# A gated recurrence on one core: the step re-ordered, and the update gate's products computed with the state as the stationary operand

## The reference

```python
vz, vr, vh = video @ C_z + b_z, video @ C_r + b_r, video @ C + b
def step(h, xs):                                  # layer 1, 256 steps in sequence
    xzt, xrt, xht = xs                            # seq @ W_z, seq @ W_r, seq @ W
    z = sigmoid(xzt + h @ U_z + vz)               # update gate
    r = sigmoid(xrt + h @ U_r + vr)               # reset gate
    hh = tanh(xht + r * h @ U + vh)               # candidate
    h_new = (1.0 - z) * h + z * hh
...
def step(h, z_t):                                 # layer 2, z_t is x + layer 1's output
    gate = sigmoid(h @ Wh.T + z_t @ Wz.T + b)
    h_new = tanh(h * (1.0 - alpha) + gate * z_t)
```

## Time and profile before

| | |
|---|---|
| Median of 3 runs | 990.21 us (986.84 to 991.89) |
| The profiled execution | 990.85 us, of which the span of the trace is 989.0 us |
| The 256 steps | from about 21 us to 612 us of the span |
| PE busy in 100 to 200 us | 99.05 us of 100 |
| DVE and ACT busy in the same stretch | 79.83 and 78.83 us |
| Mean step between 100 and 600 us | 2.252 us (222 steps in 500 us) |

### The profile page before, as it was taken

One profiled execution on the slowest core, in us unless ns is written; L12 is line 12 of the kernel. 1 busy time (PEld: TensorE's weight loads), 2 busy tenths in 40 slices (PEclk: granted clock), 3 DMA queues, 4 the chain that ended last, 5 costly groups with the idle time before them and its releaser, 6 DMA issues.

```text
span 989.0 us, 112546 instructions
## 1 busy us (share of the span) xinstructions
PE 943.0 (95%) x50966; PEld 766.4 (77%) x50966; DVE 802.5 (81%) x2372; ACT 647.3 (65%) x2862; POOL 221.2 (22%) x430
## 2 busy tenths in 40 slices
PE   6699999999999999999999999969999999999996
PEld 5699999999999999999999998335555555555554
DVE  2378778878788778777878787799999999999992
ACT  2478777777777777777777776336455556555552
POOL 0011111111111111111111111324434334434340
PEclk7699999999999999999999999979999999999998
DMA  6113312310010100100101001100011000001001
GB/s 218 41 55 112 110 50 95 111 35 27 24 37 24 37 24 27 34 27 24 37 24 37 24 27 33 28 1 25 24 37 34 24 24 24 24 31 41 24 24 43
DMA packets 38294, 42.01 MB, mean 42 GB/s; under 512 B 5120, under 2 KB 31232, under 8 KB 37120
## 3 DMA queue, kind: packets, MB, share of 16 engines
q1 hardware_dynamic: 36832, 40.55, 13.2%
q10 hardware_dynamic: 1440, 1.18, 0.4%
HBM read 32.80 MB, written 8.91 MB: 42 GB/s over the span
## 4 chain that ended last, share of the span: by engine, by line
PE 57%; DVE 29%; issue 7%; ACT 4%; DMA 1%; ACTq 1%; POOL 0%; DVEq 0%; POOLq 0%
PE bank L788 30%; PE bank L734 22%; DVE arena L667 10%; DVE early L686 4%; DVE early L677 4%; ACT cand_kept L391 2%; DVE early L690 2%; DVE early L684 2%; DVE early L671 2%; DVE early L665 2%; DVE none_h L604 2%; PE bank L906 2%; PE bank L923 1%; DMA bias<-in_bias 1%; PE bank L877 1%
## 5 line engine op out<-in xcount | busy, mean ns | idle before, releaser
L734 PE MATMUL bank<-x_ahead,early 128*32 128x64 f32 x12376 | 345.7, 224 | 5.9 <-ACT bank L358 3.2
L734 PEld LDWEIGHTS bank<-x_ahead,early 128*32 128x32 f32 x12376 | 239.7, 111 | 3.3 <-issue 3.3
L788 PE MATMUL bank<-none_h,early 128*32 128x32 f32 x16384 | 203.1, 199 | 8.8 <-issue 4.9
L280 POOL TENSOR_TENSOR x<-x_f,h_gx 128x64 f32 x256 | 87.6, 342 | 529.4 <-PE bank L788 528.3
L788 PEld LDWEIGHTS bank<-none_h,early 128*32 128x32 f32 x16384 | 180.6, 110 | 27.4 <-DVE none_h L604 13.5
L906 PE MATMUL bank<-x,wl 128*128 (+1 forms) x384 | 182.3, 614 | 0.9 <-DVE rank_rows L646 0.9
L788 PE MATMUL bank<-rh_f,early 128*32 128x32 f32 x8192 | 151.0, 199 | 5.0 <-DVE rh_f L592 2.2
L906 PEld LDWEIGHTS bank<-x,wl 128*128 128x128 f32 x384 | 69.2, 192 | 89.0 <-issue 89.0
L788 PEld LDWEIGHTS bank<-rh_f,early 128*32 128x32 f32 x8192 | 122.1, 112 | 7.0 <-DVE rh_f L592 5.0
L604 DVE TENSOR_TENSOR_SCAN none_h<-zero_z,cand_kept 128x64 f32<-128x64 f32 x512 | 121.6, 279 | 5.3 <-ACT cand_kept L391 3.9
L402 ACT ACTIVATE h_gx<-h_pre 128x64 f32<-128x64 f32 x256 | 68.7, 268 | 81.0 <-DVE h_pre L630 81.0
(11 more groups left out here) (95 smaller groups left out, 1294.4 us busy)
## 6 DMA issues: line engine op xcount, KB each, us to landing
x_in<-in_x SPq DMA_DIRECT2D x34, 256.0 KB, 2.7
x_ahead<-in_x SPq DMA_DIRECT2D x130, 64.0 KB, 1.8
arena<-in_w SPq DMA_DIRECT2D x8, 1024.0 KB, 5.6
out<-y SPq DMA_DIRECT2D x32, 256.0 KB, 2.5
rank_rows<-in_bias_rows SPq DMA_DIRECT2D x1, 1024.0 KB, 5.0
arena<-scratch SPq DMA_DIRECT2D x64, 16.0 KB
early<-in_cx SPq DMA_DIRECT2D x1, 768.0 KB, 4.5
early<-in_wx SPq DMA_DIRECT2D x1, 768.0 KB, 6.3
```

The costliest lines, as they stand in the source:

```text
L280: pool.tensor_tensor(x2[:, :, :, s], x1_f[:, u % LOOP], h1_gx[:, u % 2, :, :, 0], ALU.add).then_inc(x2_done, 1)
L734: mm = pe.matmul(out[32 * j:32 * j + 32], weights(k, j, m), moving(k), start=False, stop=False, tile_position=(0, 32 * j), skip_group_chec ...
L788: mm = pe.matmul(out[32 * j:32 * j + 32], weights(k, j, m), moving(k), start=False, stop=k == 1, tile_position=(0, 32 * j), skip_group_che ...
```

## The change

Four things change.

1. **Update gate.** For each contraction half and column group the matmul now has the state (32 batch columns) stationary and 64 columns of U_z moving, so 8 matmuls a step stand in place of 16. The x part (`ahead_update`) is turned likewise, with as many matmuls as before. The result lies with the batch in the partitions. ACT takes one sigmoid into `z_row`; DVE turns it in 32x32 blocks into `zero_z` (a transpose), and forms (z - 1) * h with one scalar_tensor_tensor. ACT's `keep_f` is gone; the candidate is computed with a negative sign, and the scan subtracts.
2. **Order on PE.** Reset products come ahead of most of the update products; the 16 matmuls of 64 columns that don't depend on the state stand between the gates and the candidate, the candidate has no `hole`, and layer 2's gate products stand after the candidate. Another 16 matmuls of 64 columns end the step.
3. **Order on DVE and ACT.** On DVE layer 2's product and sum and the previous step's x1 stand ahead of r * h. On ACT layer 2's tanh stands after z and layer 2's gate after the candidate.
4. **Waits.** r_done and cand_done are counted down by PE, so DVE waits on constants; SP's refill of x_in for the second half of a turn is issued after the second load of `x_ahead` of the next turn.

```diff
-                keep = lambda k, m: quarter(pre_z[par][:, m, v, :], w_z, state, k, m)
+                def update(k, slabs=range(SLABS)):
+                    for j in slabs:
+                        mm = pe.matmul(pre_z[par][32 * j:32 * j + 32, v], state(k), urz[:, k, j, 1, :],
+                                       start=False, stop=k == 1, tile_position=(0, 32 * j), skip_group_check=True)
+                    return mm
                 pe.wait_ge(h_done, 1)
                 reset(0, 0)
-                keep(0, 0)
-                keep(0, 1)
+                pe.wait_ge(cand_done, 2)
+                reset(0, 1)
+                update(0, range(2))
                 pe.wait_ge(h_done, 2)
-                reset(1, 0, taken=h_done).then_inc(r_pre, 1)
-                reset(0, 1)
+                reset(1, 0, taken=(h_done, cand_done)).then_inc(r_pre, 1)
                 reset(1, 1).then_inc(r_pre, 1)
-                keep(1, 0)
-                mm = keep(1, 1)
-                if late_keep:
-                    mm = late_keep()
-                mm.then_inc(z_pre, 1)
+                update(0, range(2, SLABS))
+                update(1).then_inc(z_pre, 1)
...
             def turn():
+                for u in range(LOOP):
+                    later = 1 - u // STEPS
+                    first_gates(u)
+                    if u % STEPS == 0:
+                        pe.wait_ge(ahead_loaded[later], 16)
+                        pe.wait_ge(reset_seeded, 2)
+                        ahead_first(later, 0, 0)
+                        ahead_first(later, 0, 1).then_inc(reset_seeded, -2)
+                    else:
+                        ahead_second((u - LAG) % LOOP, later)
+                    first_cand(u)
+                    second_gate(u)
+                    if u % STEPS == 0:
+                        ahead_first(later, 2, 0)
+                        ahead_first(later, 2, 1)
+                    else:
+                        ahead_update(later).then_inc(ahead_loaded[later], -16)
...
-                act.activation(zero_z[:, u % 2, :, :, 1], pre_z[par][:, :, v, :], ACT.Sigmoid).then_inc(z_done, 1)
-                act.activation(keep_f[:], pre_z[par][:, :, v, :], ACT.Sigmoid, scale=-1.0).then_inc(z_done, 1)
+                act.activation(z_row[:], pre_z[par][:, v, :], ACT.Sigmoid).then_inc(z_done, 1)
...
+            def update_state(n, u):
                 t, now = n * BODY + u, (u + 1) % 2
+                dve.wait_ge(z_done, t + 1)
+                dve.transpose(zero_z[:, u % 2, :, :, 1].rearrange("p m b -> p (m b)"), z_row[:]).then_inc(z_turned, 1)
+                dve.wait_ge(z_turned, t + 1)
+                dve.scalar_tensor_tensor(cand_kept[:, u % 2, :, :, 1], zero_z[:, u % 2, :, :, 1], 1.0,
+                                         none_h[:, now, :, :, 1], ALU.subtract, ALU.mult).then_inc(kept_done, 1)
...
             def turn(n, first=False):
                 for u in range(BODY):
+                    if not first or u > LAG:
                         second_gated(n, u)
+                        second_sum(n, u)
+                    early = not first or u > LAG
+                    if early:
+                        first_output(*((n, u - 1, first) if u else (n - 1, BODY - 1)))
+                    reset_state(u)
...
+                    update_state(n, u)
                     next_state(n, u)
```

More of the change, by code:

```diff
@@ L93, in build_program @@
         rstd = sb("rstd", [P, 1])
-        idle = sb("idle", [P, 2 * LAG])
+        idle = sb("idle", [P, LAG + 1])
         normed = sb("normed", [P, SLAB])
@@ L130, in build_program @@
         pre_rh = [[half(banks[2 * m + n]) for m in range(HALVES)] for n in range(2)]
-        pre_z = [half(banks[4 + n]) for n in range(2)]
+        pre_z = [banks[4 + n][:, 0:STEPS * SLAB].rearrange("p (v e) -> p v e", v=STEPS) for n in range(2)]
         pre_g = [half(banks[6 + n]) for n in range(2)]
@@ L215, in next_turn @@
                                  ).then_inc(ahead_loaded[c % 2], 16)
+                    if c == 3 and not first:
+                        next_steps(n - 1, 1)
                     if c == 6:
@@ L219, in next_turn @@
                         sp.dma_start(dst, src).then_inc(done, 16)
-                next_steps(n, 1)
-            next_turn(0, [(dst[:], io[name], tail_in) for dst, name in TAIL_LOADS])
+            next_turn(0, [(dst[:], io[name], tail_in) for dst, name in TAIL_LOADS], first=True)
             for w in range(4):
@@ L728, in recur, with ahead @@
                 return mm
-            def ahead(out, m, weights, moving, parts=range(HALVES)):
-                for k in parts:
+            def ahead(out, m, weights, moving):
+                for k in range(HALVES):
                     for j in range(SLABS):
@@ L736, in ahead, with ahead_update, ahead_first @@
                 return mm
-            def ahead_first(par, gate, m, parts=range(HALVES)):
-                out = (pre_rh[par][m][:, 0], pre_z[par][:, m], pre_rh[par][m][:, 1])[gate]
+            def ahead_update(par):
+                for v in range(STEPS):
+                    for k in range(HALVES):
+                        for j in range(SLABS):
+                            mm = pe.matmul(pre_z[par][32 * j:32 * j + 32, v], x_ahead[:, par, v, k, :], wx[:, k, j, 1, :],
+                                           start=False, stop=False, tile_position=(0, 32 * j), skip_group_check=True)
+                return mm
+            def ahead_first(par, gate, m):
+                out = pre_rh[par][m][:, gate // 2]
                 return ahead(out.rearrange("p v b -> p (v b)"), m,
                              lambda k, j, m: wx[:, k, j, gate, m * BLK:(m + 1) * BLK],
-                             lambda k: x_ahead[:, par, :, k, :], parts)
+                             lambda k: x_ahead[:, par, :, k, :])
             def ahead_second(at, par):
@@ L765, in _ @@
             pe.wait_ge(first_in, 16 * len(FIRST_LOADS))
-            for gate in range(3):
-                mm = recur(lambda m: pre_const[:, gate, m], lambda k, j, m: cx[:, k, j, gate, m * BLK:(m + 1) * BLK],
-                           lambda k: cond_f[:, k])
+            for gate in (0, 2):
+                recur(lambda m: pre_const[:, gate, m], lambda k, j, m: cx[:, k, j, gate, m * BLK:(m + 1) * BLK],
+                      lambda k: cond_f[:, k])
+            for k in range(HALVES):
+                for j in range(SLABS):
+                    mm = pe.matmul(pre_const[32 * j:32 * j + 32, 1].rearrange("p m b -> p (m b)"), cond_f[:, k],
+                                   cx[:, k, j, 1, :], start=False, stop=k == 1, tile_position=(0, 32 * j),
+                                   skip_group_check=True)
             mm.then_inc(const_pre, 1)
@@ L784, in _, with quarter @@
             pe.wait_ge(weights_in, 16 * len(WEIGHT_LOADS + SECOND_LOADS))
-            def quarter(out, weights, moving, k, m, taken=None):
+            def quarter(out, weights, moving, k, m, taken=()):
                 for j in range(SLABS):
```

200 lines of the change are left out of this document (86 added, 114 removed).

## The result

The changed kernel takes **1011.89 us** (median of 4 runs, 1010.16 to 1014.05) where the kernel before takes 990.15 (4 runs, 986.84 to 991.89): ratio 1.0229 (95% interval 1.0202 to 1.0257). It is slower, by more than four times what a measurement here can tell; the forecast was 983 us in a range up to 1008.

A forecast was written before the change was run, and what follows sets the result against it. It took the kernel to be bound by a dependence loop nearly as long as PE's own work; 0.033 us less a step gave 990.85 - 8.4 + 0.6 = 983.0 us, range 967 to 1008 us.

The forecast's parts named there:

- Edges: Step with PE's branch: 2.31 against 2.20 now; PE loop 2.26 there, 0.08 over the gate loop, once in four.
- the gate's loop: Candidate through layer 2's gate products, sigmoid, product, sum, x1 and r * h back to PE: 2.18 us, the longest, deciding the step.
- Three loops: Dependence loops of the changed step: gate 2.18, PE 2.16, update 2.13 us; the longest decides.
- 32 gate records: Layer 2's gate products on PE: issue taken as 0.27 us, within 0.56 us from their start to the sigmoid.
- PE's loop: PE's issue of candidate, gate, work ahead and state products, then through r and r * h back to PE: 2.16 us.
- Edges, ACT's and DVE's branch: Step where ACT and DVE branch: some 0.3 us above its neighbours, kept once in 16, 0.019 us a step.
- state-stationary products: PE's 16 update records of 64 columns: 14.7 ns each, 0.24 us; bounds 0.12 to 0.47 us.
- DVE's pieces: New DVE work: transpose 0.24 us and scalar_tensor_tensor product 0.23 us, each possibly up to 0.40.
- z comes last: Rival: transpose and product ahead of the state's scan take 0.20 us more together, 30 us lost, 1021 us; chance 0.2.
- DVE's instructions overlap by 0.08 us: Successive DVE instructions without a wait overlap 0.08 us; the no-overlap rival loses 53 us, 1044 us, chance 0.03.
- DVE's idle time ahead of the scan: Sign of wrong: DVE idle ahead of transpose or scan, instead of layer 2's product, would mean z is late.
- the loads' wait "for the state" in one step of four: Reading of the earlier list of waits: PE's loads wait for the state in one step of four.

The follow-up runs named there:

- experiment 3: Changed kernel with the old update gate (16 products of 32 columns, z straight into place, no transpose): 1005.76 us, 1.0196 to the kernel before.
- experiment 8: Kernel before with PE's loop body cut behind the state's products instead of ahead of them: 1003.42 us, 1.0166 to the kernel before.
- experiment 12: Changed kernel with x1 behind r * h, PE's branch ahead of the candidate and seeds awaited bank by bank: 989.90 us, 1.0023 to the kernel before.
- Experiment 7: Changed kernel with PE's loop body rotated so its branch lies ahead of the candidate: 999.88 us, 1.0132 to the kernel before.
- Experiment 5: Changed kernel with half of the step-ending 64-column work put between the candidate and layer 2's gate products: 1038.34 us, single run.
- experiment 9: Changed kernel with eight of the step's last 64-column products moved ahead of the candidate: 1015.46 us, 1.0276 to the kernel before.
- 10: Changed kernel, x1 behind r * h, branch ahead of candidate, eight 64-column products moved ahead except in the branch step, seeds awaited bank by bank: 982.30 us, 0.9942.
- experiments 1 and 2: PE's loop body of eight steps instead of four, in the changed kernel (1825.61 us, 1.8471) and in the kernel before (1930.87 us, 1.9556).
- experiments 4: Kernel before, in its old order, with the new form of the update gate: 990.34 us, 1.0031 to the kernel before.
- 6: Changed kernel with DVE's x1 put behind both halves of r * h: 1009.36 us, 1.0222 to the kernel before.

## Why the prediction was wrong

Step by step, in the order of the prediction. In steps of the loop, the forecast 2.219 and the measured 2.342 (the mean of the four positions) differ by 0.123 us.

- **Edges, the first failed step.** It priced PE's branch from the row where it shows, 2.31 against 2.20, and let the gate's loop cover a part: 0.08 once in four. (2.16 and 0.11 are 2.27 and not 2.26; the slip is worth 0.6 us.) But that row shows what the wait for the state left over. By the earlier trace rows the last record of work ahead starts at 404.45 + 38 x 14.7 ns = 405.01, and PE's timeline goes on at 405.29: 0.28 us without an issue. The state's first half is ready for PE at 404.81 + 0.34 = 405.15, so half of the 0.28 lay over a wait. In the changed kernel the last record ahead starts at 404.79 + 0.45 = 405.24 and the next at 405.51, again 0.27, while the state was ready at 404.83 + 0.34 = 405.17: nothing lies over it. The step pays 2.59 - 2.25 = 0.34 in place of 0.08, 0.065 a step over all, 17 us.

  Two things make up the 0.34. By medians, PE takes up the state 0.68 behind the scan there and 0.41 elsewhere, 0.27 more, the whole gap; the state's products then take 0.10 longer to reach the sigmoid of r (0.71 for 0.61); 0.03 of the two don't show in the step. The old form of the update gate in the same order (experiment 3) has the bare gap, 0.26, and not the slow products, and pays 0.24.

  The other side is experiment 8: in the old kernel, moved to a place without a wait, the branch costs 1.7%, 16 us, where I expected 3 to 9. Where half or a third of a 0.27 gap lies over a wait, as in the kernel before and in experiment 12, it shows as 0.10 and 0.13. Experiment 7 gives back 1.0%, 10 us, near the 8 expected, but by a shorter gap and not by the wait.
- **Three loops, the term "32 gate records", the second.** I took 0.27 us for their issue, as in the earlier trace rows; they take 0.36 (31 x 11.7 ns), since they now stand right behind 32 records of 32 columns. This term lies in the gate's and in PE's loop, both of which the forecast put at 2.16 to 2.18, so it shows in every ordinary step: 2.25, 0.07 or 18 us more. The gate's loop, measured piece by piece in the forecast's order (medians of ordinary steps), is 0.21 + 0.65 + 0.26 + 0.33 + 0.34 + 0.12 + 0.10 + 0.24 = 2.25: the 0.65 stands for the forecast's 0.56, all else together is 0.02 shorter than forecast. Experiment 5 shows the cause as far as the order goes: apart from the candidate they take 0.30. Why they are slow behind it stays open. That the instruction supply of PE falls behind in a long row of short matmuls was the theory, and it isn't enough: of the 64 short records from the state in the kernel before, the first 56 stand 7 to 11 ns apart and only the last eight 13, while of the 32 gate records in the changed kernel the first eight stand 8 ns apart, the next eight 19, and the rest 10 to 11.
- **A wait left out.** In even steps PE waits 0.16 us for ACT's seeds ahead of `ahead_first`: 2.28 against 2.25, 2 us. Small here, but it ate experiment 9 and the wait that experiment 7 was to use; with the seeds waited for bank by bank (experiment 12) even steps are as long as odd ones.
- **Edges, ACT's and DVE's branch.** The 0.3 us once in 16 that I kept isn't seen apart from PE's branch step: 0.019 a step or 5 us too much.

Sum: 0.065 + 0.07 + 0.0075 - 0.019 = 0.123. The terms are differences of medians; the remaining 4 us between 983 + 256 x 0.123 = 1014.5 and the 1010.16 of the profiled run lie in the start, where the first scan comes at 19.36 us for 21.13, and in the early steps: the first 32 take 88.3 us for 88.8, where 32 x 0.09 = 2.9 more were due.

What held: the state-stationary products run near the pitch of other 64-column ones (the last 12 of a step 16 ns apart, for the 14.7 of the forecast), DVE's pieces cost 0.246 and 0.227 us, z was never last, and DVE's instructions overlap by 0.08 us as before. The slower rival "z comes last" gave a time of the right sign for a reason that didn't occur. The Trainium skill (VectorE: DVE Perf Modes, The DRAIN you can't avoid) has the next operation wait until the pipe is empty, but says in the same place that one which is not held starts earlier. The rows are of the second kind: in the changed kernel too x1 starts at 403.75 with 0.20 us and `rh_f` at 403.86, 0.09 ahead of its end.

What the forecast named as a sign against itself did come: DVE's idle time ahead of the scan, though not for z. x1 starts 0.35 behind the sum, and the product right behind the gate's sigmoid, as they should if the gate's loop binds. One reading of the earlier trace rows was wrong from the start: the loads' wait "for the state" in one step of four is the branch, and the step without one that does wait, 0.14 us, isn't on the list.

Where the expected gain went: the new form pays only where PE's loop is the longest. In the new order as changed, the gate's loop and the branch held the step. With those mended (10) it is worth 2.2%, and the kernel is 0.6% faster than the kernel before.

**Open.** In the new form the state products right behind the branch come more slowly, which makes that step 0.10 longer than in the old form (2.59 against 2.49, experiment 3). Why, no run tells. Nor does one tell why the gap at the branch is 0.27 in most places, 0.16 in experiment 7 and 0.39 in experiment 8. That the gap is the branch and not something else at the end of the body is shown by its moving with it in experiments 7 and 8 (the old place keeps 0.006 us in the one, and in the other 0.14, the wait for the state that other steps have too); experiments 1 and 2, which should have halved it, tell nothing.

## What to carry to other kernels

A row that shows what a stall costs shows only what the waits beside it left over: before moving code at a loop's edge, measure the gap in the issue itself (here 0.28 us, of which 0.10 showed) and ask what lies over it in the new place, in that very step: an idle time seen in odd steps is no cover in an even one. Then put the branch where the engine waits anyway, and measure the gap again, since it changed with the place. A pitch belongs to a neighbourhood: the same 32 records stand 8.4 ns apart behind wide ones and 11.7 behind 32 narrow ones. When several loops lie within 0.05 us, a mend of one alone shows little or the wrong sign, as experiments 4, 6 and 9 did here; they must be tried together, and then each left out in turn.

## What was not expected of the hardware

- A PE loop body of eight steps makes the kernel 1.85 and 1.96 times as long, with pauses of up to 3.9 us and 0.88 MB through an instruction queue in 200 us; a body of four steps has no such row in the same stretch, at 15059 records of PE for 6401.
- PE's branch leaves 0.27 and 0.28 us without an issue in the two kernels, 0.16 in experiment 7, and 0.39 in the median of experiment 8; what the difference is, no run tells.
- 32 records of 32 columns slow from 8.4 to 11.7 ns apart right behind 32 others from another operand, while 56 of 64 from the state keep 7 to 11 ns.
